# Layer 1 experts of a perceiver kernel: dense over all eight experts, or tokens listed by expert, gathered and scattered

## What is computed

```python
def _L1_ffn_ref(x, Wr, br, W1, b1, W2, b2):
    router_logits = x @ Wr + br
    expert_idx = jnp.argmax(router_logits, axis=-1)
    onehot = jax.nn.one_hot(expert_idx, NUM_EXPERTS, dtype=x.dtype)
    h = jax.nn.gelu(jnp.einsum('bsd,edh->bseh', x, W1) + b1, approximate=False)
    y = jnp.einsum('bseh,ehd->bsed', h, W2) + b2
    out = jnp.einsum('bsed,bse->bsd', y, onehot)
    return out
...
    x = x + _L1_ffn_ref(_layernorm(x, axis=-1), L1_ffn_Wr, ...)
```

## Time and profile before

| | us |
|---|---|
| median of 3 runs | 4973.83 |
| the profiled execution | 4967.2 |
| its span, first to last instruction | 4965.4 |
| TensorE, matmuls busy in the span | 3806.3 |
| VectorE busy | 2819.0 |
| ScalarE busy | 2343.4 |
| GpSimd busy | 1435.7 |
| layer 1 experts stage, from the last `WT` copy (2158.9) to the last add (2524.1) | 365.2 |

### The profile page before, as it was taken

One profiled execution on the slowest core, in us unless ns is written; L12 is line 12 of the kernel. 1 busy time (PEld: TensorE's weight loads), 2 busy tenths in 40 slices (PEclk: granted clock), 3 DMA queues, 4 the chain that ended last, 5 costly groups with the idle time before them and its releaser, 6 DMA issues. The chain is left out here.

```text
span 4965.4 us, 93741 instructions
## 1 busy us (share of the span) xinstructions
PE 3806.3 (77%) x28449; PEld 2730.1 (55%) x28449; DVE 2819.0 (57%) x6493; ACT 2343.4 (47%) x6756; POOL 1435.7 (29%) x1102
## 2 busy tenths in 40 slices
PE   1675957588999866789979999677865276859986
PEld 1554942266777656467757777422323243727764
DVE  4776646455777679212237777589993412435553
ACT  1333431387777634434446666444442014537763
POOL 0220010001565554000015555366660050105420
PEclk9887966799999889879989999899996586979988
DMA  5000000122222100000001111133332024900000
GB/s 177 7 6 9 0 4 1 32 80 64 66 68 66 45 6 0 5 26 0 0 15 30 30 30 30 59 128 128 132 115 71 10 33 120 224 12 0 0 1 21
DMA packets 165118, 229.69 MB, mean 46 GB/s; under 512 B 58786, under 2 KB 130381, under 8 KB 162134
## 3 DMA queue, kind: packets, MB, share of 16 engines
q1 hardware_dynamic: 159342, 223.67, 15.4%
q0 software_dynamic: 5632, 4.33, 0.7%
HBM read 201.64 MB, written 9.45 MB: 43 GB/s over the span
## 5 line engine op out<-in xcount | busy, mean ns | idle before, releaser
L2794 PE MATMUL l2a_pY<-l2a_hc,ident 128*128 128x512 f32 x512 | 271.5, 661 | 129.6 <-DVE l2a_hc L2919 129.6
L2687 POOL TENSOR_TENSOR l2a_dbu<-l2a_dx,l2a_BC 128x1024 f32<-128x1024 f32 x128 | 300.8, 2353 | 155.5 <-DVE l2a_pH L2912 143.4
L2258 ACT ACTIVATE l2x_att_prob<-l2x_att_pS,l2x_att_nmx 128x257 f32<-128x257 f32 x512 | 236.0, 474 | 209.4 <-DVE l2x_att_nmx L2294 209.4
L2912 DVE TENSOR_TENSOR_SCAN l2a_pH<-l2a_pA,l2a_dbu 128x512 f32<-128x512 f32 x256 | 300.0, 1217 | 44.7 <-POOL l2a_dbu L2687 34.4
L2114 POOL TENSOR_TENSOR l2x_att_prob<-l2x_att_prob,l2x_att_rs 128x1028 f32<-128x1028 f32 x128 | 243.1, 1899 | 274.0 <-DVE l2x_att_rs L2299 274.0
L2258 ACT ACTIVATE l1x_att_prob<-l1x_att_pS,l1x_att_nmx 128x257 f32<-128x257 f32 x512 | 236.0, 474 | 147.8 <-DVE l1x_att_nmx L2294 147.6
L2114 POOL TENSOR_TENSOR l1x_att_prob<-l1x_att_prob,l1x_att_rs 128x1028 f32<-128x1028 f32 x128 | 243.2, 1900 | 206.7 <-DVE l1x_att_rs L2299 206.7
L2811 ACT ACTIVATE l2a_pA<-l2a_dl,l2a_A 128x512 f32<-128x512 f32 x256 | 176.2, 691 | 260.4 <-DVE l2a_pH L2912 256.8
L2794 PEld LDWEIGHTS l2a_pY<-l2a_hc,ident 128*128 128x128 f32 x512 | 96.2, 203 | 298.0 <-DVE l2a_hc L2919 203.8
L2310 DVE COPY l1x_att_probT<-l1x_att_pT 86x512 f32<-86x512 f32 x256 | 175.6, 686 | 115.6 <-PE l1x_att_pT L2200 107.2
L2310 DVE COPY l2x_att_probT<-l2x_att_pT 86x512 f32<-86x512 f32 x256 | 175.9, 687 | 107.6 <-PE l2x_att_pT L2200 107.6
(11 more groups left out here) (686 smaller groups left out, 10047.7 us busy)
## 6 DMA issues: line engine op xcount, KB each, us to landing
l2a_BC<-l2a_rows SPq DMA_DIRECT2D x128, 512.0 KB, 3.6
l3x_att_ctn<-ctx_n SPq DMA_DIRECT2D x32, 576.0 KB, 14.4
l0x_sum_ctx<-ctx_t SPq DMA_DIRECT2D x16, 1028.0 KB, 4.8
l1x_k_xin<-ctx_t SPq DMA_DIRECT2D x32, 514.0 KB, 3.5
l1x_att_ctx<-ctx_t SPq DMA_DIRECT2D x128, 128.5 KB, 2.1
l1x_att_kT<-l1x_KA SPq DMA_DIRECT2D x128, 128.5 KB, 2.2
l2x_att_ctx<-ctx_t SPq DMA_DIRECT2D x128, 128.5 KB, 2.1
l3x_att_ctx<-ctx_t SPq DMA_DIRECT2D x32, 514.0 KB, 12.6
```

The costliest lines, as they stand in the source:

```text
L2258: last = act.activation(prob[:, b, j, 0:KEYS], pS[:, j, 0:KEYS], ACT.Exp, bias=nmx[:, b, j:j + 1], accum_out=sums[:, b, j:j + 1])
L2687: pool.tensor_tensor(dbu[:, u % 2], dx[:, g % 2], bc(BC[:, u % RING, 0, :], 1, NC), ALU.mult).then_inc(dbu_made, 1)
L2794: last = pe.matmul(pY[c][:, :], env.ident[:, :], hc[:, u % 2, c, :], start=False, stop=n == NS - 1)
L2912: dve.tensor_tensor_scan(pH[c][:, :], pA[c][:, :], dbu[:, u % 2, c, :], 0.0, ALU.mult, ALU.add).then_inc(h_made, 1)
```

## The change

Layer 1's feed-forward is computed by expert instead of by token. The weights are fetched before the normalisation, into buffers of the outer stage, with the biases laid out as single rows. `normalise` also writes its table. `route` gets no `WT`, and its last loop is left out. A new stage, `list_by_expert`, counts the tokens of each expert, rounds each expert up to whole tiles of 128 (at most 32 + 7 = 39 tiles), and makes for each tile the rows to gather (`at`), the rows to scatter to (`to`, unused lanes going to spare rows past the end) and the offset of its expert's weights (`first`). A second new stage, `top_experts`, runs the 39 tiles, always all of them. TensorE reads `first` into a register for each tile. The tokens are stationary in the first layer now, so the bias is a matmul of a row of ones, and the hidden values have to be turned over. Results are scattered to HBM, read back in four parts and added to `X`.

```diff
-                for g in range(GROUPS):
+                for g in range(GROUPS if WT is not None else 0):
                     act.wait_ge(w_turned, g + 1)
...
+def list_by_expert(nc, env, title, W, at, to, first):
+    NT = TOP_TILES + 1
...
+                for d, s_ in ((tri, env.a.c_upto), (lanes_f, env.a.c_lanes), (tiles_f, env.a.c_tiles),
+                              (row_f, env.a.c_row)):
+                    sp.dma_start(d[:, :], s_).then_inc(loaded, 16)
+                sp.dma_start(later[:, :, :].rearrange("p e n -> p (e n)"), env.a.c_later).then_inc(loaded, 16)
...
+                pe.matmul(pt[:, 0:H], env.ones[:, 0:P], weights).then_inc(totals, 1)
+                pe.matmul(pp[:, 0:H], tri[:, :], weights).then_inc(prefixes, 1)
+                pe.wait_ge(hot, 1)
+                for n in range(TILES):
+                    last = pe.matmul(pl[:, 0:3 * NT], hot_lo[:, n, :], by[:, n].rearrange("p a j -> p (a j)"),
+                                     start=n == 0, stop=n == TILES - 1)
...
+                then(dve.tensor_tensor_scan(flat(cum), flat(later), flat(tot), 0.0, ALU.mult, ALU.add))
...
+                then(dve.tensor_tensor(by[:, :, 2, :], bc(hi[:, :], 2, NT), bc(tiles[:, :], 1, TILES), ALU.is_equal))
+                dve.tensor_scalar(by[:, :, 0, :], by[:, :, 2, :], row_f[:, 0:1], None, ALU.mult)
+                dve.tensor_tensor(by[:, :, 1, :], by[:, :, 2, :], bc(tiles[:, 0:TILES], 2, NT), ALU.mult)
+                dve.tensor_tensor(hot_lo[:, :, :], bc(lo[:, :], 2, P), bc(lanes[:, :], 1, TILES), ALU.is_equal
+                                  ).then_inc(hot, 1)
...
+def top_experts(nc, env, title, w, fetched, table, at, to, first, out):
+    C, RING = 3, 4
...
+                def gather(j):
+                    done(pool, turned, j - RING)
+                    pool.indirect_dma_start(xg[:, j % RING, :], None, table,
+                                            bass.IndirectOffsetOnAxis(ap=at[:, j:j + 1], axis=0)
+                                            ).then_inc(landed[j % RING], 16)
+
+                def scatter(j):
+                    done(pool, y_kept, j)
+                    pool.indirect_dma_start(out, bass.IndirectOffsetOnAxis(ap=to[:, j:j + 1], axis=0),
+                                            y[:, j % RING, :], None).then_inc(stored[j % RING], 16)
+
+                for j in range(RING):
+                    gather(j)
+                for j in range(TOP_TILES):
+                    scatter(j)
+                    if j + RING < TOP_TILES:
+                        gather(j + RING)
...
+                for r in range(RING):
+                    sp.wait_ge(stored[r], 16 * ((TOP_TILES - 1 - r) // RING + 1))
+                rows = out[0:T, :].rearrange("(p n) d -> p n d", n=TILES)
+                for k in range(PARTS):
+                    sp.dma_start(back[:, k * PER:(k + 1) * PER, :], rows[:, k * PER:(k + 1) * PER, :]
+                                 ).then_inc(returned, 16)
+                    sp.wait_ge(returned, 16 * (k + 1))
+                    sp.sem_inc(added, 1)
...
+                def turn(j):
+                    pe.wait_ge(landed[j % RING], 16 * (j // RING + 1))
+                    done(pe, x_kept, j - 2)
+                    pe.transpose(pT[j % 2][:, 0:P], xg[:, j % RING, :], env.ident[:, :]).then_inc(turned, 1)
+
+                def hidden(j):
+                    f = pe.value_load(first[0:1, j:j + 1], min_val=0, max_val=(EXPERTS - 1) * C * P)
+                    done(pe, x_kept, j)
+                    done(pe, h_kept, j - 2)
+                    h = pH[j % 2][:, 0:C * P]
+                    pe.matmul(h, env.ones[0:1, 0:P], w.b1[0:1, bass.ds(f, C * P)], start=True, stop=False)
+                    pe.matmul(h, xT[:, j % 2, :], w.w1[:, bass.ds(f, C * P)], start=False, stop=True).then_inc(h_made, 1)
+                    return f
+
+                def turn_hidden(j):
+                    done(pe, h_kept, j)
+                    done(pe, u_kept, j - 2)
+                    for c in range(C):
+                        last = pe.transpose(pU[j % 2][:, c * P:(c + 1) * P], hid[:, j % 2, c * P:(c + 1) * P],
+                                            env.ident[:, :])
+                    last.then_inc(u_made, 1)
+
+                def output(j, f):
+                    done(pe, y_kept, j - 2)
+                    o = pY[j % 2][:, 0:D]
+                    pe.matmul(o, env.ones[0:1, 0:P], w.b2[0:1, bass.ds(f, D)], start=True, stop=False)
+                    done(pe, u_kept, j)
+                    for c in range(C):
+                        last = pe.matmul(o, hidT[:, j % 2, c * P:(c + 1) * P], w.w2[:, bass.ds(f + c * P, P)],
+                                         start=False, stop=c == C - 1)
+                    last.then_inc(y_made, 1)
+
+                turn(0)
+                f = {}
+                for j in range(TOP_TILES + 2):
+                    if j + 1 < TOP_TILES:
+                        turn(j + 1)
+                    if j < TOP_TILES:
+                        f[j] = hidden(j)
+                    if j >= 2:
+                        output(j - 2, f.pop(j - 2))
+                    if 0 < j <= TOP_TILES:
+                        turn_hidden(j - 1)
...
+                    act.activation(hid[:, j % 2, :], pH[j % 2][:, 0:C * P], ACT.Gelu).then_inc(h_kept, 1)
...
+                def yield_(j):
+                    done(dve, y_made, j)
+                    if j >= RING:
+                        dve.wait_ge(stored[j % RING], 16 * (j // RING))
+                    dve.tensor_copy(y[:, j % RING, :], pY[j % 2][:, 0:D]).then_inc(y_kept, 1)
...
+                for k in range(PARTS):
+                    dve.wait_ge(added, k + 1)
+                    x = env.X[:, k * PER:(k + 1) * PER, :]
+                    dve.tensor_tensor(x, x, back[:, k * PER:(k + 1) * PER, :], ALU.add)
...
 def l1_ffn(nc, env, a):
-    normalise(nc, env, "l1f_ln", env.X, dst_t=env.XNT)
...
-        WT = st.sb("WT", [EXPERTS, T])
-        route(nc, env, "l1f_route", (a.L1_ffn_Wr, a.L1_ffn_br), W, WT, "one")
-        w = Names(w1=a.L1_ffn_W1, b1=a.L1_ffn_b1, w2=a.L1_ffn_W2, b2=a.L1_ffn_b2)
-        gelu_experts(nc, env, "l1f_exp", w, EXPERTS, 3, W=W, WT=WT)
...
+                for d, s_ in ((w.w1, a.L1_ffn_W1), (w.b1, a.L1_ffn_b1), (w.w2, a.L1_ffn_W2), (w.b2, a.L1_ffn_b2)):
+                    sp.dma_start(d[:, :], s_).then_inc(fetched, 16)
+        normalise(nc, env, "l1f_ln", env.X, dst_t=env.XNT, table=table.rearrange("(p n) d -> p n d", n=TILES))
+        route(nc, env, "l1f_route", (a.L1_ffn_Wr, a.L1_ffn_br), W, None, "one")
+        list_by_expert(nc, env, "l1f_list", W, at, to, first)
+        top_experts(nc, env, "l1f_exp", w, fetched, table, at, to, first, out)
```

More of the change, by code:

```diff
@@ L739, in l1_ffn, with _ @@
 def l1_ffn(nc, env, a):
-    normalise(nc, env, "l1f_ln", env.X, dst_t=env.XNT)
+    table = nc.dram_tensor("l1f_table", (T, D), F32).ap()
+    out = nc.dram_tensor("l1f_out", (T + (TOP_TILES + 1) * P, D), F32).ap()
     with stage(nc, "l1f") as st:
         W = st.sb("W", [P, TILES, EXPERTS])
-        WT = st.sb("WT", [EXPERTS, T])
-        route(nc, env, "l1f_route", (a.L1_ffn_Wr, a.L1_ffn_br), W, WT, "one")
-        w = Names(w1=a.L1_ffn_W1, b1=a.L1_ffn_b1, w2=a.L1_ffn_W2, b2=a.L1_ffn_b2)
-        gelu_experts(nc, env, "l1f_exp", w, EXPERTS, 3, W=W, WT=WT)
+        at, to = st.sb("at", [P, TOP_TILES + 1], I32), st.sb("to", [P, TOP_TILES + 1], I32)
+        first = st.sb("first", [1, TOP_TILES + 1], I32)
+        EC = EXPERTS * 3
+        w = Names(w1=st.sb("w1", [P, EC * P]), b1=st.sb("b1", [1, EC * P]), w2=st.sb("w2", [P, EC * D]),
+                  b2=st.sb("b2", [1, EC * D]))
+        fetched = st.sem("fetched")
+        with nc.Block() as block:
+            @block.sync
+            def _(sp):
+                for d, s_ in ((w.w1, a.L1_ffn_W1), (w.b1, a.L1_ffn_b1), (w.w2, a.L1_ffn_W2), (w.b2, a.L1_ffn_b2)):
[4 more added lines that the diff above has]
+        top_experts(nc, env, "l1f_exp", w, fetched, table, at, to, first, out)
@@ L3376, in layouts @@
     o["L1_attn_b2"] = row("L1_attn_b2")
-    o["L1_ffn_Wr"], o["L1_ffn_br"], o["L1_ffn_b2"] = v["L1_ffn_Wr"], row("L1_ffn_br"), v["L1_ffn_b2"]
-    o["L1_ffn_W1"], o["L1_ffn_b1"], o["L1_ffn_W2"] = mlp(v["L1_ffn_W1"], v["L1_ffn_b1"], v["L1_ffn_W2"])
+    o["L1_ffn_Wr"], o["L1_ffn_br"] = v["L1_ffn_Wr"], row("L1_ffn_br")
+    o["L1_ffn_W1"], _, o["L1_ffn_W2"] = mlp(v["L1_ffn_W1"], v["L1_ffn_b1"], v["L1_ffn_W2"])
+    o["L1_ffn_b1"] = v["L1_ffn_b1"].reshape(1, -1)
+    o["L1_ffn_b2"] = np.concatenate([v["L1_ffn_b2"]] * 3, axis=1).reshape(1, -1)
     o["L2_ffn_norm_weight"] = col("L2_ffn_norm_weight")
@@ L3458, in more_constants @@
     c["row"] = np.arange(P).reshape(P, 1)
+    c["upto"] = tok[:, None] <= tok[None, :]
+    c["lanes"] = np.tile(tok, (P, 1))
+    c["tiles"] = np.tile(np.arange(TOP_TILES + 1), (P, 1))
+    c["later"] = np.tile(np.arange(TILES) > 0, (P, EXPERTS))
```

(2 more changed lines are left out.)

126 lines of the change are left out of this document (added).

## The result

The changed kernel takes 5065.99 us (median of 4 runs, 5055.95 to 5075.7), the kernel before beside it 4975.62: 1.82% slower, ratio 1.0182 [1.016, 1.0205]. Its profiled execution took 5055.95 us, span 5054.1. The forecast was 5045 (4955 to 5105), slower.

What follows compares the result with a forecast made beforehand. TensorE's matmuls were taken to bound the replaced stage. Experts 408.5, listing 29.7 and front 5.5, less 372.1 removed, gave +71.6 on 4967.2: 5038.8 profiled, 5045 us as median (4955 to 5105).

Steps and rivals of the forecast that it cites:

- TensorE's arithmetic isn't the limit, the order is: New expert stage: TensorE's work for 39 tiles is 122 us at full clock; waits in queue order set the time.
- the ring does hide the gathers: Expert loop: four buffers cover the gathers, cycle 6.26 us at the slow clock, total 4905 us; chance 0.03.
- The cycle of 10.27 us: Expert loop: copy, scatter, gather, landing and TensorE's work follow one another; 35 cycles of 10.27 us, 359.5 us.
- The register read, 0.5: Expert loop: TensorE's load of a tile's weight offset, priced at 0.5 us for each of 39 tiles.
- The sum: Whole kernel: 408.5 + 29.7 + 5.5 - 372.1 = +71.6 us, giving 5038.8 for the profiled execution.
- dear read: Expert loop: the register read costs 1.7 us instead of 0.5, 47 us more, total 5092 us; chance 0.09.
- The slow clock: Expert stage: TensorE stands still about 4 us every cycle, so the slow level (0.51 in layer 2) was taken throughout.
- full-clock rival: Expert stage: full clock holds over 4 us of idleness, cycle 8.05 us, total 4957 us; chance 0.11.
- The start: Expert stage, from the first gather to the end of output 0, ahead of the 35 cycles: 16.3 us.
- the tail: Expert stage after the 35 cycles: last three outputs, copy, scatter, landing, four read-backs and last add, 32.7 us.
- The listing stage: `list_by_expert`, ahead of the experts and wholly on the path: about 29.7 us (22 to 40).
- The front: Before the listing: issuing four weight transfers, 3.2 us, and landing of the normalise table, 2.3; together 5.5 (2 to 10).

Runs made afterwards that it cites:

- gather first: Changed kernel with two lines of GpSimd's loop swapped, so gather(j+4) is issued ahead of scatter(j); 4898.2 us, ratio 0.9849 to the kernel before.
- 128-row bias: Changed kernel with both bias matmuls using 128 rows (ones against the bias padded with zero rows) instead of one; 5022.4 us, ratio 1.0106 to the kernel before.
- The filler: Changed kernel plus five unread f32 matmuls of 384 columns after turn_hidden in 35 iterations; 4999.5 us, ratio 1.0048 to the kernel before.

## Why the prediction was right, step by step

The forecast for the profiled execution was 5038.8; it took 5055.95, 17 more. Direction, bound and rank of the rivals held; single terms were off.

- *TensorE's arithmetic isn't the limit, the order is.* Shown: two different edits of the order gave 165 us each. The rival "the ring does hide the gathers" had been priced at 6.26 us per tile and 4905 us; with the order mended, "gather first" measured 6.31 and 4898. That it met so closely is partly luck, since its errors cancel: `hidden` was 0.60 longer than its price and `output` 0.09, the register read cost nothing there (transpose to bias 0.35 instead of 0.78), and three transposes took 0.64 instead of 0.85.
- *The cycle of 10.27 us.* In the kernel 35 cycles took 386.0 us (2198.98 to 2584.94), 11.03 each; forecast 359.5. This is the term that was mis-sized. By its parts, as means of the 35 cycles: copy and way to GpSimd 0.57 (0.61); scatter with its issue 1.29 (1.55), the accumulate being the difference; gather and landing 2.75 (2.7); transpose to bias 0.86 (0.78); `hidden` 3.15 (2.56); `output` with the next copy's start 2.41 (2.07). The scatter was too dear by 0.26, TensorE's part too cheap by 1.01. So two errors partly cancelled; without the scatter's the cycle would have been 1.0 too short instead of 0.76.
- *Where the 1.01 was.* I priced matmuls by columns: four of 384, eight of 128. The switches between one-row and 128-row weights are in no such price; with the 128-row bias `hidden` is 0.43 shorter and `output` about 0.46, at the same slow level. Layer 2 has a one-row bias ahead of each group of output matmuls, and I took the group alone.
- *The register read, 0.5.* Measured with its addressing: 0.46 in a cycle by the rows, 17 us in the stage. The sum had it about right. I had also said 39 times; it counts only where TensorE had waited just before. The rival "dear read" (1.7) is out.
- *The slow clock.* Right, 0.50 in the whole stage; but for a reason that was only half of it. I argued from the standing still, and it does play a part: with 128 rows in both, the grant in TensorE's busy time was 0.54 with the waits and 0.94 with most of them gone. Yet with no standing still at all ("gather first") the grant stayed at 0.50, so in this kernel the one-row products, or the switches that come with them, kept it there too. The full-clock rival at 8.05 us per cycle and 4957 was thus further away than I gave it. The filler, at 0.81 to 0.86, took 1.9 us off the cycle; the rival had 2.22 for the whole step to 1.
- *The start* took 18.0 us (16.3), *the tail* 32.3 (32.7), in it the read-backs 3.9 to 4.1 each with the next issue (3.8). By its own terms the stretch of the last three outputs adds up to 11.8, not the 12.4 that I wrote; it took 12.1.
- *The listing stage*: 27.1 us (29.7). The 4096-element compare took 4.42 (4.9), the 32 matmuls 3.38, between the bounds of 1 and 4.5, of which the sum took the upper. *The front*: from the last add of the block before to the end of `W` it was 60.1 us and is 62.4, 2.3 more (5.5).
- *The sum*: cycles +26.5, start +1.7, tail -0.4, listing -2.6, front -3.2, and, where I had counted nothing, -0.4 ahead of the front and -4.6 behind the experts, which is within what those blocks vary by: +17. Without these 5 us the miss would have been 22. The median is 10 above this execution, not 6.6, which makes the 21 us to the forecast.

The rule of the Trainium skill on issuing early and waiting late ("DMA: Bandwidth & Descriptors", rules for kernel authors) was drawn on in the prediction for the ring. The runs agree with it, with a supplement: what counts is the distance in the queue. One place further gave 165 us; two buffers more, at the full clock, 51.

## What to carry to other kernels

Where a gather, work and a scatter share one in-order queue, write down which of them must end before the next gather may start, and count the iterations between; a ring of four was no ring at all here because the scatter stood ahead of the gather, and swapping two lines gained 3.3%. Less arithmetic (TensorE's busy time in the stage fell from 308 us at full clock to 258 at half) is worth nothing while the new order is a sum. Once the waits are out, look at what the engine is busy with: here a one-row bias product cost more time in the loop than one padded to 128 rows, and the clock as well. And read the granted clock over the engine's busy time: a mean over its waits can rise without the work getting faster.
